# Two deformable 3x3 convolutions on one core: five taps gathered and four dense, with hats for 32 rows spread by one-hot matmuls, against seven gathered and two dense

## What is computed

```python
def deform(feat, w, b, w_off, b_off):           # feat: 64 channels, 32x32
    off = conv3x3(feat, w_off, b_off)            # dy, dx of 9 taps (L1 also: mask = sigmoid)
    ys = row + ky + dy ; xs = col + kx + dx
    sampled = bilinear(feat, ys, xs)             # 4 corners, weights (1-|y-ys|)+ * (1-|x-xs|)+ , times mask
    return einsum('nckhw,ock->nohw', sampled, w) + b
```

## Time and profile before

| | |
|---|---|
| three runs | 266.61, 268.70, 271.57 us; median 268.7 us |
| profiled execution | 269.83 us; its span 268.0 us |
| TensorE busy | 210.7 us (79%), 808 records; mean granted clock 0.877 |
| VectorE, ScalarE, GpSimd busy | 158.3, 117.9, 136.0 us |

### The profile page before, as it was taken

The page is one execution under the profiler, slowest core; times in us unless marked ns, Lnnn a source line. Parts: engine busy times, 40 slices in busy tenths (PEclk is TensorE's granted clock), DMA queues, the critical chain, the costliest instruction groups (busy, mean ns, idle before and its releaser), DMA issues. The chain is left out here.

```text
span 268.0 us, 2403 instructions
## 1 busy us (share of the span) xinstructions
PE 210.7 (79%) x808; PEld 109.6 (41%) x808; DVE 158.3 (59%) x270; ACT 117.9 (44%) x159; POOL 136.0 (51%) x127
## 2 busy tenths in 40 slices
PE   8999987787979568196997979489876764999920
PEld 7364963543333223034873746233332231343500
DVE  2965537766867954844166466567476676352271
ACT  2120335786686837001206148848738551023231
POOL 6000017877878877870010077788777787720010
PEclk9999995678899999677799975979899998699965
DMA  7400113323233232230000223223323223310004
GB/s 257 171 0 2 39 41 98 98 86 93 80 99 93 83 98 80 79 98 21 0 2 0 78 66 110 78 83 95 98 78 97 81 80 97 100 39 0 0 0 157
DMA packets 8654, 19.80 MB, mean 74 GB/s; under 512 B 1985, under 2 KB 4162, under 8 KB 8514
## 3 DMA queue, kind: packets, MB, share of 16 engines
q0 software_dynamic: 5376, 14.69, 18.0%
q1 hardware_dynamic: 3122, 4.44, 4.8%
q10 hardware_dynamic: 144, 0.52, 0.5%
HBM read 17.55 MB, written 2.10 MB: 73 GB/s over the span
## 5 line engine op out<-in xcount | busy, mean ns | idle before, releaser
L321 POOL DMA_INDIRECT G<-table,idx x112 | 129.1, 1153 | 58.1 <-issue 47.7
L558 DVE TENSOR_TENSOR GW<-G,corner_w 128x1024 f32<-128x1024 f32 (+1 forms) x32 | 34.9, 1091 | 52.0 <-DMA G<-table,idx 51.1
L951 PE MATMUL ps<-first,GS 128*128 128x128 f32 x64 | 15.5, 328 | 37.1 <-DVE GS L573 37.0
L753 ACT ACTIVATE sT<-ps 128x256 f32<-128x256 f32 x32 | 12.2, 381 | 64.0 <-PE ps L951 64.0
L906 PE MATMUL ps<-x,V 128*64 128x512 f32 x64 | 38.4, 731 | 0.0
L723 ACT ACTIVATE near_y<-ps,dbias 128x1024 f32<-128x1024 f32 x32 | 35.4, 1106 | 1.5 <-PE ps L898 1.5
L308 POOL TENSOR_TENSOR rstd<-var,half_neg 64x1 f32<-64x1 f32 (+1 forms) x4 | 2.6, 638 | 64.0 <-DVE var L371 42.2
L726 ACT ACTIVATE hat_y<-near_y 128x1024 f32<-128x1024 f32 x32 | 33.8, 1057 | 1.0
L799 PE MATMUL ps<-first 128*128 128x128 f32 x180 | 28.6, 316 | 0.0
L799 PEld LDWEIGHTS ps<-first 128*128 128x128 f32 x180 | 25.7, 224 | 4.2 <-issue 3.9
L951 PEld LDWEIGHTS ps<-first,GS 128*128 128x128 f32 x64 | 7.1, 153 | 45.0 <-DVE GS L573 43.7
(11 more groups left out here) (132 smaller groups left out, 235.1 us busy)
## 6 DMA issues: line engine op xcount, KB each, us to landing
G<-table,idx POOLq DMA_INDIRECT x112, 2.9
second<-in_second SPq DMA_DIRECT2D x1, 1552.5 KB, 8.6
table<-feat_t SPq DMA_DIRECT2D x4, 256.0 KB, 2.3
out<-x SPq DMA_DIRECT2D x4, 256.0 KB, 2.2
x<-in_x ACTq DMA_DIRECT2D x1, 512.0 KB, 4.6
x<-in_x SPq DMA_DIRECT2D x1, 512.0 KB, 5.4
first<-in_first SPq DMA_DIRECT2D x1, 224.0 KB, 4.4
at_w<-in_w_b SPq DMA_DIRECT2D x1, 1.0 KB
```

Of the source, the lines that this page charges most:

```text
L321: pool.indirect_dma_start(out=G[:, done % RING, k, :], out_offset=None, in_=table[b], in_offset=bass.IndirectOffsetOnAxis(ap=idx[b][:, n:n ...
L558: dve.tensor_tensor(GW[:, :, k0:k1].rearrange("p c k e -> p k c e"), G[:, (b * TILES + t) % RING, k0:k1].rearrange("p k (c e) -> p k c e", ...
L753: act.activation(sT[:, t % 2, 2 * part:2 * part + 2], ps[:, B_ST[part], 0:2 * P] .rearrange("p (q n) -> p q n", n=P), ACT.Copy).then_inc(s ...
L951: mm = pe.transpose(ps[:, B_ST[part], q % 2 * P:(q % 2 + 1) * P], GS[:, t % 2, k:k + 2, :].rearrange("p k e -> p (k e)"), ident)
```

## The change

Five taps are gathered in place of seven, and four are dense in place of two. Parts:

- Gathers: 8 x 5 = 40 in a stage, one unit per tile (8 in place of 16), a ring of four `G` tiles. VectorE's three operations and the transposes and contractions work on a whole tile of 5 taps (3 pairs in place of 4).
- Hats: the y hat of a tap depends only on the source row (32 values), the x hat only on the source column. They are computed once for 32 rows as 128-partition tiles that hold two taps or two axes: Y, XA, XB, C, D (and MY, MS, the sigmoids, for b = 0). Each is a `fill` (two f32r matmuls with `sel`), a `distance` (Abs) and a `hat_of` (Relu) on ScalarE. The row hats are split in a high and a low part (`sign_rows` on ScalarE, `high_and_low` on VectorE) into the f32r tiles `duo`.
- Two taps by products: per chunk TensorE spreads the 32 row hats over 128 source pixels by a one-hot f32r matmul into PSUM (`spread_product`, K = 64), VectorE multiplies by `hat_x`, TensorE adds with V as before (`add_product`).
- Two taps by squares: 2ab = (a+b)^2 - a^2 - b^2. TensorE spreads the sum of both hats (`spread_square`, K = 128), ScalarE squares it, TensorE adds with V/2 (`add_square`); the squares are taken off with `correct` (four f32 matmuls a stage, weights `CW` from eight small matmuls).
- Offsets: bias, ramp and base come into the offset matmul by one more f32r matmul of K = 4 for each half; VectorE's additions (L481) go. `to_pixels` is a matmul with `pick` in place of a transpose.
- Loops: `BESIDE`, `PREPARE`, `LAG` and the keep-clock matmuls inside the loop go; `PROD_AT` and `SQUARE_AT` place 16 product and 16 square chunks.

```diff
-DENSE = 2
-GTAPS = TAPS - DENSE
-PARTS = [(0, 4), (4, GTAPS)]
-BESIDE = [0, 0, 1, 1, 2, 1, 1, 2, 1, 1, 2, 1, 1, 2, 0, 0]
+GTAPS = 5
+PAIRS = GTAPS // 2 + 1
+PROD = 2
+SQUARE = 2
+PROD_AT = [3, 3, 2, 2, 2, 2, 2, 0]
+SQUARE_AT = [2, 3, 3, 3, 3, 2, 0, 0]
+LATE_TILE = 2
+CORRECT_AT = [1, 4]
...
+                def spread_product(c):
...
+                    if done:
+                        pe.wait_ge(s_prod, done)
+                    for h in range(2):
+                        mm = pe.matmul(ps[:, B_P + h, :], spread[rows, i, t], half(duo["Y"], h)[rows],
+                                       start=True, stop=True)
+                    mm.then_inc(s_bp, 1)
+
+                def spread_square(c):
...
+                    for h in range(2):
...
+                        pe.matmul(ps[:, B_S + h, :], spread[:, i, t], half(duo[name], h),
+                                  start=True, stop=True).then_inc(s_bs, 1)
+
+                def add_product(c):
...
+                    for h in range(2):
...
+                        mm = pe.matmul(ps[0:HID, B_C1 + h, :], V[:, t, i, :], half(SP[done % PRING], h),
+                                       start=(c == 0), stop=last)
...
+                for u in range(TILES + 1):
+                    products = list(at(PROD_AT, u))
+                    squares = list(at(SQUARE_AT, u))
+                    if u == LATE_TILE:
+                        pe.wait_ge(s_sq, 2 * (b * SQUARE_CHUNKS + squares[0]))
+                        fill("D")
+                        pe.wait_ge(s_reads, fills_s(b, "D") + 1)
+                    if u in CORRECT_AT:
+                        correct(CORRECT_AT.index(u))
+                    for j in range(max(len(products), len(squares), 1)):
+                        if j < len(products):
+                            spread_product(products[j])
+                        if j < len(squares):
+                            spread_square(squares[j])
+                        if j < len(products) and products[j]:
+                            add_product(products[j] - 1)
+                        if j < len(squares) and squares[j]:
+                            add_square(squares[j] - 1)
+                        if j == 0 and u >= 1:
+                            turn(u - 1)
+                        if j == 0 and u >= 2:
+                            contract(u - 2)
...
             def samples(b):
...
+                distance(b, "Y")
+                hat_of(b, "Y")
+                if b == 0:
+                    modulation("MY")
+                pixel_hats(b)
+                distance(b, "XA")
+                hat_of(b, "XA")
+                sign_rows(b, "Y")
+                distance(b, "C")
+                hat_of(b, "C")
+                if b == 0:
+                    modulation("MS")
+                distance(b, "XB")
+                hat_of(b, "XB")
+                sign_rows(b, "C")
+                for t in range(TILES):
...
+                    for c in at(SQUARE_AT, t):
+                        square(b, c)
```

More of the change, by code:

```diff
@@ L120, in conv_chain @@
         split = sb("split", [P, PW, PW], F32R)
-        offw = [sb(f"offw{b}", [P, TAPS, 4, SLOT], F32R) for b in range(2)]
+        offw = [sb(f"offw{b}", [P, TAPS + 1, 4, SLOT], F32R) for b in range(2)]
+        aux_own = sb("aux", [P, N], F32R)
+        aux = aux_own[HID:HID + 4]
         om_sb = sb("om_sb", [2 * SLOT, N])
@@ new lines, in _ @@
+            dve.tensor_tensor(as_rows(aux), fld["ramp"][HID:HID + 4, None, 0:W].to_broadcast([4, H, W]),
+                              fld["ramp"][HID:HID + 4, W:2 * W, None].to_broadcast([4, H, W]),
+                              ALU.add).then_inc(s_aux, 1)
+            def offset_operands(b):
+                w = fld[f"b{b + 1}off"].rearrange("p (t o) -> p t o", o=OM)
+                then(dve.tensor_copy(offw[b][:, :, 0, 0:OM], w))
+                dve.tensor_tensor(offw[b][:, :, 1, 0:OM], w, offw[b][:, :, 0, 0:OM].bitcast(F32),
@@ L640, in _ @@
             act.activation(warm[:], zeros[0:H, 0:1], ACT.Sigmoid)
+            act.wait_ge(s_first, 16)
+            for side in range(2):
+                rows = slice(side * HID, (side + 1) * HID)
+                for variant in range(2):
+                    place = spread[rows, variant].rearrange("p t (r x) -> p (t r) x", x=W)
+                    eye = fld["eye"][rows]
+                    act.activation(place, (eye[:, None, :] if side != variant else eye[:, :, None])
+                                   .to_broadcast([HID, H, W]), ACT.Copy).then_inc(s_spread, 1)
             act.wait_ge(s_const, 1)
@@ new lines, in add_square, with correct @@
+                def add_square(c):
+                    i, t = divmod(c, TILES)
+                    for h in range(2):
+                        done = 2 * (b * SQUARE_CHUNKS + c) + h
+                        pe.wait_ge(s_sq, done + 1)
+                        pe.matmul(ps[0:HID, B_C1 + h, :], V[:, t, PROD + i, :], half(SS[c % SRING], h),
+                                  start=False, stop=False).then_inc(s_mains, 1)
+                def correct(i):
+                    name = "CD"[i]
+                    pe.wait_ge(s_cw, SQUARE * b + SQUARE)
+                    pe.wait_ge(s_hatsq, SQUARE * b + i + 1)
+                    for h in range(2):
+                        pe.matmul(ps[0:HID, B_C1 + h, :], CW[:, i], half(full[FULL[name]], h),
+                                  start=False, stop=False)
@@ new lines, in turn @@
+                def turn(t):
+                    done = b * TILES + t
+                    pe.wait_ge(s_gs, done + 1)
+                    if done >= 2:
+                        pe.wait_ge(s_sT, done - 1)
+                    for q in range(PAIRS):
+                        k = min(2 * q, GTAPS - 2)
+                        mm = pe.transpose(ps[:, B_ST[t % 2], q * P:(q + 1) * P],
+                                          GS[:, t % 2, k:k + 2, :].rearrange("p k e -> p (k e)"), ident)
+                    mm.then_inc(s_st, 1)
@@ new lines, in deform @@
+                fill("Y")
+                if b == 0:
+                    fill("MY")
+                taps_of_pixels(1)
+                fill("XA")
+                fill("C")
+                if b == 0:
+                    pe.wait_ge(s_sums, 4)
+                    pe.wait_ge(s_sig, 2)
+                pe.wait_ge(s_VD, b + 1)
+                for t in range(TILES):
+                    mm = pe.matmul(ps[:, B_SMALL, CW_AT:CW_AT + SQUARE * HID],
+                                   sums[:, t].rearrange("p g j -> p (g j)"),
+                                   V[:, t, PROD:].rearrange("p d e -> p (d e)"),
+                                   start=(t == 0), stop=(t == TILES - 1))
```

689 lines of the change are left out of this document (374 added, 315 removed).

## The result

The changed kernel takes 337.88 us in the median of four runs (336.19 to 339.36), the kernel before 267.97 us beside it: ratio 1.263, 95% interval 1.252 to 1.274. The forecast was 329 us, with a range of 306 to 353. The profiled execution took 338.95 us, its span 337.1 us.

What follows compares the result with a forecast made beforehand. The prediction took GpSimd's gathers to bound the kernel before and TensorE's loop after; stages adding 30.5 and 30.1 us, plus 0.3, raised the 268.0 us span to 328.9, so 329 us was forecast, range 306 to 353.

Steps and rivals of the forecast that it cites:

- Gathers no longer end last: GpSimd in each stage: 40 gathers take 58 us, less than TensorE's 88.5 us loop, so they stop setting the end.
- TensorE's loop: First square spread to last adding: 32 chunks at 2.35 us plus corrections, fill of D, turns and contractions, 88.5 us a stage.
- The clock at the start: Start of each stage's loop: TensorE arrives after little work at a low clock, losing 2.0 us a stage, between 0 and 4.
- The head: Ahead of each loop: nothing hides the preparation of the hats, so the first square spread comes at 60.0 (b = 0).
- the end of the offset matmuls: Before the first fill: previously at 37.55, now 1.3 us later (0.8 to 1.8) for added matmuls and records.
- the way from there to the first fill: From offset matmuls to first fill: 4.0 us, as VectorE's two additions go, putting the fill at 42.9.
- ScalarE's list: Between first fill and first square spread: ScalarE's distances, hats, signs, sigmoids and short operations in order, 14.4 us for b = 0.
- without a gap: Sign for the head: ScalarE works from the first distance to the second sign with no idle time between.
- The tails: Behind each stage's last adding: statistics or residuals, turns and contractions, 6.0 us for b = 0 and 8.8 for b = 1.
- Rival 1: In the loop, every spread matmul pays its weight load, 10.2 us more a stage, time 350; chance 0.15.
- Rival 2: In the loop, spreads wait for the consumers of earlier chunks, 17 us more a stage, time 364; chance 0.12.
- Rival 3: TensorE fits the new matmuls into its waiting time, each stage ends 23.2 us earlier, time 222; chance 0.03.

Runs made afterwards that it cites:

- e4: Changed kernel with two more gathers per tile, data unused (56 a stage again), and three G tiles in place of four: 339.35 us in a single run.
- e1: Changed kernel with every dense chunk's adding in f32r in place of f32, and fewer G and product buffers: 270.3 us in the median.
- e5: Changed kernel with added matmuls ahead of the loops that only keep TensorE busy, to hold its clock: 335.2 us, ratio to before 1.250.
- e6: Changed kernel with the first three product chunks ahead of the first square, and duo C made after two products: 332.5 us, ratio to before 1.244.
- e7: Changed kernel with f32r addings and products first, the edits of e1 and e6 together: 265.1 us, ratio to before 0.988.
- e2: Changed kernel with every spread matmul issued twice with the same operands: 363.1 us in a single run.
- e3: Changed kernel without adding the 16 square chunks of each stage to the sum, spreads and squares still made: 297.3 us in a single run.
- e10: e7 with D's sign rows after its tile's second square, D's low part made before the tile's additions, and the second correction later: 258.1 us.
- e9: Kernel before, with its 32 dense matmuls a stage in f32r and three S tiles in place of four: 268.6 us, ratio 0.998.
- e8: e7 with five clock-keeping matmuls ahead of the XB fill (b = 0) and five behind it: 264.4 us in the median.
- e11: The kernel of e10 run again with more rounds for an interval: 259.6 us, ratio to before 0.957.

## Why the prediction was right
The mechanism was right: TensorE's loop is the path and the gathers are not. By its own steps, and what each measured. The first stage of the changed kernel takes 6.6 us more than forecast, the second 3.9 more, and the rest 2.3 less: 328.9 + 6.6 + 3.9 - 2.3 = 337.1. The 2.3 less, and some 2 us of the 6.6, differ from one execution to the next and cancel by luck.

- *Gathers no longer end last.* Right. They wait for VectorE, and e4 puts 16 of them back a stage for 1.5 us.
- *TensorE's loop.* Right in kind and near in size. From first square spread to last adding 94.7 us in both stages, against 88.5 + 2.0. Two chunks took 4.89 where the sum had 4.70: a pair of spreads costs 0.66, the upper end of its 0.50 to 0.65, where 0.58 had been taken, and the second adding 1.81. On 32 chunks that is 3.0 us a stage. e1 shows the addings' share by taking it out.
- *The clock at the start.* 3.5 us in place of 2.0 (three pairs at 1.15, an adding at 3.46, part of the next), inside the 0 to 4. e5 took it away in the loop of b = 0, and in part in b = 1.
- *The head.* The loop started at 63.76, not 60.0. This is the term that missed by most. 1.1 us of it is the end of the offset matmuls, at 40.0 (39.2 to 39.7 in the other traces of this code). Another 2.1 is the way from there to the first fill: 6.1 us, not 4.0. It is the clock: from 40.67 to 46.09 the granted clock is 0.50, `to_pixels(1)` takes 1.73 us and the 16 records of `taps_of_pixels(0)` 3.69, so that the fill comes 1.3 us after its `om_split` is there. The same 16 records stood ahead of the first fill in the kernel before too, at full clock:

```profile
38.54 2.00 PE L876 MATMUL ps<-second,feat 64*128 64x128 f32 x16
```

  In the traces of e1, e4, e6 and e7 the same instructions find the full clock at first (`to_pixels(1)` takes 0.9 us), the fill waits for `om_split`, and the way is 4.2 us; over all traces of this head it is 4.2 to 6.1. So the 4.0 was a fair size at full clock, and the prediction had no term for a fall of the clock there. Why it falls at 40.67 in one execution and later in another stays open. ScalarE's list took 17.7 from fill to spread against 17.1. The sign "without a gap" did not come: ScalarE waited 1.62 us (2.06 for b = 1) for the fill of XA, which stands behind `taps_of_pixels(1)`, 16 records more than the kernel before had and none of them in the sum; its operations of 1.00 to 1.06 us, where the sum has 1.106 and 1.057, gave most of that back. For b = 1 the way to the first fill was 4.0 as forecast and the whole head 19.7 against 18.4. e6 shows that the head delays the end: an earlier start shortened the two stages by 1.8 and 5.8 us.
- *The tails.* 4.9 against 6.0 (b = 0), 8.8 against 8.8 (b = 1).
- *What was not in the sum.* After the full loop the following group norm finds TensorE at full clock: sixteen matmuls take 2.05 us at 163.35, where they took 3.78 in the kernel before. The way from the last contraction of b = 0 to the end of the second offset matmuls was 1.6 us shorter than forecast. The span ends 22.9 us after the last contraction, not 25.2. None of this lies in the work: ScalarE's last instruction ends 19.7 us after that contraction (19.4 in the kernel before). Behind it, while the last outputs land, the span goes on for 3.2 us here, for 5.8 in the kernel before, and for 5.8 in e4 too, whose code is the same there; what decides it is not shown.
- *Rival 1, spreads pay their loads.* Half right in e2: 0.2 us once a pair, which the forecast had mostly inside it.
- *Rival 2, hand-offs.* Wrong here: no wait but the 0.78 and 1.11 us around D in either loop after its start. Right elsewhere: with fewer or cheaper addings (e3, e7) exactly these hand-offs appear, and e10 gains 5 to 7 us by moving them.
- *Rival 3, gathers still end last.* Wrong: an adding stayed at 1.77 us. With f32r (e1) the loop of 54 us is near the 58 us that this rival named for no change, and the time is no change.

## What to carry to other kernels
Work that lies beside another engine's has a price all the same, and it is due when the cover goes: the f32 addings of a stage cost nothing beside its gathers (e9: f32r in their place, and the same time), while 32 of them at 1.77 us and 32 pairs of spreads at 0.66 were 78 us of bare path. Before moving work from one engine to a second, add up start-to-start times of the second, type by type; here 16 gathers fewer a stage (23 us of GpSimd at 1.45 each) stood against 28 us more of f32 adding (16 x 1.77) and 21 us of spreading (32 x 0.66) on TensorE. When a bound is then taken away (f32r), look at once for the waits it had covered. And before an earlier start is put down to an edit, compare the two traces ahead of the edited place: here 2.6 of 4.6 us were there already.

## What the runs showed that had not been expected
- The granted clock followed the load without the time following the clock: in e9 it fell from 0.87 to 0.64 in the stages, with the time unchanged to 0.2%.
- Some kernels between full and paced TensorE had wide runs: e1 262.5 to 273.6 and e8 258.4 to 265.8, ordered by the granted clock, while the changed kernel and e9 stayed within 1%. It is no rule: e7, as much in between, stayed within 0.6%, and the runs of e11 do not order by it (258.6 us at 0.877, 260.5 and 260.7 at 0.880).
- A group of f32r spreads between f32 addings opens with 0.2 us, with K = 64 or 128 and with two matmuls or four in it (e2). In e1, where the addings are f32r too, the four pairs take 0.66, 0.57, 0.46 and 0.56 us, so the opening is not the same for every group.
- The same head, with the same code, reached its first fill between 43.4 and 46.1 us in the traces, by when TensorE's clock fell in it.
